# Dense columns stepped group by group, with two copies of the node features

## The reference

```
w  = edge_weight and 1 for each self loop
wn = w * rsqrt(deg_out[s]) * rsqrt(deg_in[d])
h  = x
repeat 10 times:                      # "steps"
    h = 0.9 * segment_sum(h[s] * wn, d) + 0.1 * x
x1 = layernorm(x + h)
score = exp(clip(sum_per_head(K[src] * Q[dst] * E / sqrt(8)), -5, 5))
out = layernorm(x1 + segment_sum(V[src] * score, dst))
```

## Time and profile before

| | |
|---|---|
| profiled execution | 13848.15 us |
| its span | 13846.3 us |
| median of the runs | 13851.04 us |
| TensorE (PE) busy | 73% of the span |
| GpSimd (POOL) busy | 64% |
| VectorE (DVE) busy | 41% |
| DMA read and written | 3177.87 MB and 303.14 MB |

### The profile page before, as it was taken

How to read it: one execution, slowest core, us unless ns; L and a number is a source line. 1 busy time by engine, 2 the same in 40 slices (tenths; PEclk the granted TensorE clock), 3 DMA queues, 4 the chain that set the end, 5 groups by cost and what they waited for, 6 DMA issues and landing times.

```text
span 13846.3 us, 141202 instructions
## 1 busy us (share of the span) xinstructions
PE 10055.4 (73%) x48612; PEld 5626.1 (41%) x48612; DVE 5672.0 (41%) x18837; ACT 688.7 (5%) x2111; POOL 8874.1 (64%) x8640
## 2 busy tenths in 40 slices
PE   0199994877868778688686886867868676777667
PEld 0199991332323323233232332333323355555555
DVE  6188881342333333333333333332333434444444
ACT  0033330000000000000000000000000010000000
POOL 3678887666666666666666666666666646666555
PEclk5555556988979889799797997989979855555555
DMA  9963335988969879699696996979969643333333
GB/s 394 385 165 69 69 54 174 374 296 310 375 228 374 328 273 375 227 375 363 236 376 231 373 374 225 373 265 336 377 228 374 249 110 108 113 109 110 106 105 97
DMA packets 1722567, 3491.10 MB, mean 252 GB/s; under 512 B 820288, under 2 KB 836067, under 8 KB 1721846
## 3 DMA queue, kind: packets, MB, share of 16 engines
q1 hardware_dynamic: 1145060, 2896.46, 56.9%
q0 software_dynamic: 379456, 296.48, 9.9%
q10 hardware_dynamic: 197330, 289.05, 5.8%
HBM read 3177.87 MB, written 303.14 MB: 251 GB/s over the span
## 4 chain that ended last, share of the span: by engine, by line
PE 55%; issue 15%; DVE 14%; another core or an unknown queue 8%; ACTq 5%; POOL 1%; ACT 1%; DMA 1%; DVEq 0%; SPq 0%
PE banks L1977 39%; PE banks L1996 5%; ACTq L1495 5%; PE banks L1946 4%; DVE arena L1673 2%; DVE arena L1737 2%; PE banks L1947 2%; PE banks L2067 1%; PE banks L2043 1%; DVE arena L1851 1%; PE banks L1989 1%; POOL dense L1460 1%; ACT arena L1504 1%; DVE arena L1687 1%
## 5 line engine op out<-in xcount | busy, mean ns | idle before, releaser
L1471 POOL DMA_INDIRECT arena<-node_rows,src_idx x5880 | 5623.7, 956 | 3174.3 <-issue 1655.0
L1977 PE MATMUL banks<-arena,u_sb 128*64 128x512 f32 x19600 | 5680.6, 625 | 1481.9 <-issue 1248.3
L1977 PEld LDWEIGHTS banks<-arena,u_sb 128*64 128x64 f32 x19600 | 1765.4, 142 | 4722.1 <-issue 4699.1
L1752 DVE TENSOR_TENSOR arena<-banks,arena 128x104 f32<-128x104 f32 (+20 forms) x1030 | 259.5, 257 | 5356.9 <-remote 4728.4
L1486 POOL DMA_INDIRECT arena<-kv_rows,src_idx x1568 | 1581.8, 1009 | 1136.8 <-DVEq L1910 553.0
L1737 DVE TENSOR_SCALAR arena<-banks,rel,w_tab 128x128 f32<-128x128 f32 x5880 | 1963.5, 403 | 166.5 <-issue 100.5
L1460 POOL DMA_INDIRECT dense<-arena x980 | 1633.5, 1667 | 591.9 <-issue 246.6
L1946 PE MATMUL banks<-arena 128*128 128x98 f32 x3136 | 1140.8, 467 | 694.8 <-ACT arena L1504 694.8
L1996 PE MATMUL banks<-arena 128*64 128x128 f32 x11760 | 1039.2, 301 | 661.6 <-issue 425.7
L1996 PEld LDWEIGHTS banks<-arena 128*64 128x64 f32 x11760 | 794.3, 149 | 925.0 <-issue 721.3
L1946 PEld LDWEIGHTS banks<-arena 128*128 128x128 f32 x3136 | 848.9, 331 | 702.9 <-ACT arena L1504 702.8
(11 more groups left out here) (166 smaller groups left out, 5382.1 us busy)
## 6 DMA issues: line engine op xcount, KB each, us to landing
arena<-dense SPq DMA_DIRECT2D x4900, 512.0 KB
dense<-blank ACTq DMA_DIRECT2D x5, 50176.0 KB, 371.2
arena<-in_dst_dram SPq DMA_DIRECT2D x195, 512.0 KB
arena<-node_rows,src_idx POOLq DMA_INDIRECT x5880
arena<-in_edge_attr_dram SPq DMA_DIRECT2D x195, 256.0 KB
u_sb<-key_rows SPq DMA_DIRECT2D x25, 1280.0 KB
u_sb<-in_edge_weight_dram SPq DMA_DIRECT2D x25, 1280.0 KB
arena<-key_rows SPq DMA_DIRECT2D x24, 1280.0 KB
```

Source lines behind the costliest of these rows:

```text
L1471: gp.indirect_dma_start(out=rows_in[:, n % ROWS, s, :], out_offset=None, in_=node_rows[k % 2], in_offset=bass.IndirectOffsetOnAxis(ap=src_ ...
L1977: last = mm(banks[h * D:(h + 1) * D, g, :], u_sb[:, j * D:(j + 1) * D], ring[:, u % SLOTS, h * 512:(h + 1) * 512], start=m < GROUPS, stop= ...
```

## The change

The dense part becomes 960 tiles and 4864 columns: four groups of 1024 columns and one of 768, of which only 768 columns are cleared, loaded and multiplied. The gathered part becomes 608 tiles, eight for each of 76 iterations. The ring has 14 slots, gathers may run 5 iterations ahead, the adds of setup go in 6 chunks, and the 490 units are spread over 74 of the 76 iterations. Units go group by group: all 98 blocks of group 0, then of group 1, and so on; each group sums in one of two banks in turn. Updates write a second copy of the features (`u_other`; the copies change places after every step), so a group is copied, turned and updated in the iteration after its last unit: iterations 15, 30, 45, 60 and 74. Within a group the blocks go 0 to 31, 38 to 97, and 32 to 37 last. ScalarE copies one bank for each group. Two waits for the adds of setup are new ahead of the steps, on GpSimd and on VectorE.

```diff
-DENSE_TILES = 980
-DENSE_COLS = 5120
+DENSE_TILES = 960
+DENSE_COLS = 4864
-TPI = 6
-SLOTS = 18
-ROWS = 7
-DENSE_ITERS = 84
+TPI = 8
+SLOTS = 14
+ROWS = 5
+DENSE_ITERS = 74
-CHUNKS = 7
+CHUNKS = 6
...
+    WIDTH = [min(GROUP, DENSE_COLS - g * GROUP) for g in range(GROUPS)]
-    dense_sum = carve(GROUPS, 512)
+    dense_sum = carve(2, 512)
+    u_other = carve(NB * D)
+    u_of = [u_sb[:, :], u_other]
...
-    GROUP_AT = {DENSE_ITERS + 2 * g: g for g in range(GROUPS)}
+    LAST_BLOCKS = list(GROUP_BLOCKS[-1])
+    BLOCK_AT = [b for b in range(NB) if b not in LAST_BLOCKS] + LAST_BLOCKS
+    UNIT = [(g, j) for g in range(GROUPS) for j in BLOCK_AT]
     UNIT_AT = [n * DENSE_ITERS // UNITS for n in range(UNITS)]
-    BLOCK_AT = [(i + DENSE_BLOCKS) % NB for i in range(NB)]
+    GROUP_AT = {UNIT_AT[(g + 1) * NB - 1] + 1: g for g in range(GROUPS)}
... run_sp
-                sp.dma_start(ring[:, n % SLOTS, :], dense_v[at:at + P, :]).then_inc(unit_loaded[n % SLOTS], 16)
+                sp.dma_start(ring[:, n % SLOTS, 0:WIDTH[g]], dense_v[at:at + P, 0:WIDTH[g]]).then_inc(unit_loaded[n % SLOTS], 16)
... run_pool, and the same in run_dve
+        for s in range(STREAMS):
+            pool.wait_ge(added[s], 16 * ROUNDS)
... run_act
-                    act.wait_ge(unit_used, (k + 1) * UNITS)
-                    for g in range(GROUPS):
-                        nc.scalar.activation(dense_sum[:, g, :], banks[:, g, :], ACT.Copy).then_inc(sum_copied, 1)
+                for turn, g in GROUP_AT.items():
+                    if turn <= i and g == copied:
+                        nth = k * GROUPS + g
+                        act.wait_ge(unit_used, k * UNITS + (g + 1) * NB)
+                        if nth >= 2:
+                            act.wait_ge(sum_turned, nth - 1)
+                        nc.scalar.activation(dense_sum[:, nth % 2, :], banks[:, nth % 2, :], ACT.Copy).then_inc(sum_copied, 1)
+                        copied += 1
... run_dve, update
-            u3 = by_node(u_sb, j0, j0 + m)
+            u3, new3 = by_node(u_of[k % 2], j0, j0 + m), by_node(u_of[(k + 1) % 2], j0, j0 + m)
-            return v.tensor_tensor(u3, part, o3, ALU.mult)
+            return v.tensor_tensor(new3, part, o3, ALU.mult)
... run_pe
-                    if k and m < GROUPS:
-                        pe.wait_ge(sum_read, (k - 1) * GROUPS + g + 1)
+                    if m % NB == 0 and nth >= 2:
+                        pe.wait_ge(sum_read, nth - 1)
-                        last = mm(banks[h * D:(h + 1) * D, g, :], u_sb[:, j * D:(j + 1) * D], ring[:, u % SLOTS, h * 512:(h + 1) * 512],
-                                  start=m < GROUPS, stop=m >= UNITS - GROUPS, tile_position=(0, h * D), skip_group_check=True)
+                        c = min(512, WIDTH[g] - h * 512)
+                        last = mm(banks[h * D:(h + 1) * D, nth % 2, 0:c], u_of[k % 2][:, j * D:(j + 1) * D], ring[:, u % SLOTS, h * 512:h * 512 + c],
+                                  start=m % NB == 0, stop=m % NB == NB - 1, tile_position=(0, h * D), skip_group_check=True)
```

More of the change, by code:

```diff
@@ L1048, in __init__ @@
         self.blank_set = sem("blank_set")
-        self.dense_cleared = [sem(f"dense_cleared{g}") for g in range(DENSE_COLS // GROUP)]
+        self.dense_cleared = [sem(f"dense_cleared{g}") for g in range(-(-DENSE_COLS // GROUP))]
         self.flag_ready = sem("flag_ready")
@@ L1085, in fast @@
     DENSE_BLOCKS = DENSE_COLS // P
+    assert DENSE_BLOCKS * P == DENSE_COLS and WIDTH[-1] > 512
+    GROUP_BLOCKS = [range(8 * g, min(8 * g + 8, DENSE_BLOCKS)) for g in range(GROUPS)]
     FIRST_BLOCK = BASE[DENSE_TILES // 2] // P
     LATE = DENSE_BLOCKS - FIRST_BLOCK
+    assert GROUP_BLOCKS[-1][0] <= FIRST_BLOCK < DENSE_BLOCKS
     assert ITERS * TPI == TILES - DENSE_TILES and ITERS % 2 == 0 and DENSE_TILES % 2 == 0
@@ L1317, in fast @@
     for n, (kind, i, what) in enumerate(UPDATES):
-        for b in (what if kind == "tail" else range(what * 8, what * 8 + 8)):
+        for b in (what if kind == "tail" else GROUP_BLOCKS[what]):
             UPDATED_AT[b] = n
-            last_use = max(UNIT_AT[m] for m in range(UNITS) if BLOCK_AT[m // GROUPS] == b)
-            assert last_use <= i - (kind == "dense")
     assert len(UPDATED_AT) == NB
@@ L1511, in run_act @@
         for k in range(STEPS):
[L1512 to L1515, removed]
+            to, u_new = node_rows[(k + 1) % 2], u_of[(k + 1) % 2]
+            copied = 0
             for n, (kind, i, what) in enumerate(UPDATES):
[L1517 to L1521 removed]
+                for turn, g in GROUP_AT.items():
[6 more added lines that the diff above has]
+                        copied += 1
                 if k + 1 == STEPS:
@@ L1757, in run_dve, with update @@
         step = Chain(dve, step_vec, fin.n)
-        def update(part, j0, m):
-            u3 = by_node(u_sb, j0, j0 + m)
+        def update(k, part, j0, m):
+            u3, new3 = by_node(u_of[k % 2], j0, j0 + m), by_node(u_of[(k + 1) % 2], j0, j0 + m)
             x3 = by_node(x_sb, j0, j0 + m)
@@ L1766, in update @@
             step(v.scalar_tensor_tensor(part, x3, ALPHA, part, ALU.mult, ALU.add))
-            return v.tensor_tensor(u3, part, o3, ALU.mult)
+            return v.tensor_tensor(new3, part, o3, ALU.mult)
+        for s in range(STREAMS):
+            dve.wait_ge(added[s], 16 * ROUNDS)
         hot_windows(0)
@@ L1788, in run_dve @@
                     if len(late) < len(done):
-                        last = update(parts[:, len(late):len(done), :], done[len(late)], len(done) - len(late))
+                        last = update(k, parts[:, len(late):len(done), :], done[len(late)], len(done) - len(late))
                         last.then_inc(updated, 1)
@@ L1797, in run_dve @@
                     dve.wait_ge(sum_turned, k * GROUPS + g + 1)
[L1798 to L1801, removed]
-                        step(v.tensor_tensor(part[:, b0:8, :], part[:, b0:8, :], carry[:, :, :], ALU.add))
-                    last = update(part, g * 8, 8)
+                    j0, m = GROUP_BLOCKS[g][0], len(GROUP_BLOCKS[g])
+                    part = banks[:, (k * GROUPS + g) % 2, 0:m * D].rearrange("p (j f) -> p j f", f=D)
+                    if g == GROUPS - 1:
+                        step(v.tensor_tensor(part[:, FIRST_BLOCK - j0:m, :], part[:, FIRST_BLOCK - j0:m, :], carry[:, :, :], ALU.add))
+                    last = update(k, part, j0, m)
                     last.then_inc(updated, 1)
-                    dve.wait_ge(updated, k * len(UPDATES) + UPDATED_AT[g * 8] + 1)
+                    dve.wait_ge(updated, k * len(UPDATES) + UPDATED_AT[j0] + 1)
                     dve.sem_inc(sum_read, 1)
```

22 lines of the change are left out of this document (13 added, 9 removed).

## The result

The kernel after took 14133.4 us (median of four runs, 14118.2 to 14143.5) beside 13848.7 for the kernel before: ratio 1.021 [1.020, 1.022]. The forecast was 12890 us, faster. The profiled execution had a span of 14133.2 us.

What follows compares the result with a forecast made beforehand. The prediction saw the bound pass from the loads to GpSimd's gathers: 2203.4 setup, nine steps of 791, a last one of 791 - 3.9, and 2774.7 behind gave 12884 us of span, forecast 12890; 8-in-10 range 12770 to 13190.

Steps and rivals of the forecast that it cites:

- setup: Ahead of the steps: 960 adds on GpSimd take 2034 us, so the first gather of step 0 comes at 2203.
- nine turns of a step: From first gather to first gather: 767 us of gathers, 6 of slip and 18 at the end, 791 us each.
- what lies behind: From the last update of step 9 to the kernel's end: 2774.7 us, untouched by the change.
- The step that failed: TensorE within a step: 7.0 us an iteration at 0.96 clock against 10.1 us of gathers, so not a bound.
- Start of a step: After the first gather: TensorE held until about 66 us, then catches up; GpSimd waits 6 us for room.
- slow spell: Some 20 us after gathers restart: TensorE's single matmuls 2.8 us apart for 47 us, cause unknown, expected at the same place.
- End of a step: After the last gather: its landing, three iterations and the stores, 18 us where the old wait is 34.
- DMA work: Loads, gathers and stores of one step on the DMA engines: 751 us before, 719 after.
- Gathers: GpSimd in each step: 608 gathers at 1.262 us make 767 us, a floor above the DMA work.
- Comparison with before: The old step of 883.2 us, read as a load-bound stretch of 725 plus a turn and a slow spell.
- B: Rival: a second slow spell in each step, 47 us more, 13360 us in all; chance 0.06.
- C: Rival: TensorE stays at its lower clock, 13.4 us an iteration at 0.50, 15000 us in all; chance 0.04.

Runs made afterwards that it cites:

- c1: The kernel before, unchanged, run again in the second set: 12336.9 us, beside 12331.7 us for the kernel before.
- c2: The kernel after, unchanged, run again in the second set: 12324.2 us, ratio 0.9993 to the kernel before.
- e14: The kernel after with 4 gathers instead of 8 in each iteration after the first five: 11136 us, 0.903 of the kernel before.
- e8: The kernel after with every unit's matmuls cut in eight, 64 columns each: 12763 us, beside 12330.7 us for the kernel before.

## Why the prediction was wrong

The sum of 12884 us of span against 14133.2, term by term: setup +8 (2203, 2211.7); nine turns of a step 9 x (914.0 - 791) = +1107; the last step 902 - 787 = +115; what lies behind +19. The error is in the step.

- **The step that failed: "TensorE. ... an iteration ... 7.0 us ... Not a bound at that clock."** The 7.0 us are right between the stretches, but three iterations take 35.0 us, 11.7 each, above the gathers' 10.1. I had divided busy rows by their count and left out what stood between them. The kernel before had the same 0.7 us gaps in every other iteration; its mean of a unit came from rows without gaps. Its steady part had them in this row, 105 us without a named cause in 700 (window 4960:5660):

```profile
L1977 PE MATMUL banks<-arena,u_sb 128*64 128x512 f32 x1859 | 526.2, 616 | 112.0 <-issue 105.1
```

There the loads, at a DMA share of 0.99, covered most of them. From the 26th to the 401st unit of a step (by the records, mean of steps 1 to 8) the kernel before takes 564 us with stretches and 535 without (c1), the kernel after 661 and 572 (c2): 30 us lost before, 88 after. The change took this cover away, and TensorE with its stretches, not GpSimd, set the pace.

- **Start of a step**: the slow spell stayed where it was, 45 us. But its slip of 6 us assumed that TensorE catches up at 7.0 us an iteration; GpSimd lost 131 us a step for room.
- **End of a step**: 31.9 us of waiting in each turn instead of 18, because TensorE is iterations behind. In c2, where it isn't, 18.5.
- **DMA work**, 719 us: too high. In e14 a step with loads as the bound takes 664; 304 gathers fewer explain 30 of the 55 (by my estimate of 0.099 us each). It decided nothing.
- **Gathers** (767) and **setup** (2203): right, 1.26 us each and 2211 us. In c2 the whole step is 783.9 for 791.
- **Comparison with before**: 883 us were taken as what loads and turn need. c1 needs 782.6 for the same program. In steps 1 to 8 the stretches cost the kernel before 103 us a step: 42 ahead of the 26th unit, 34 from there to the last one, 27 behind it. So even where my step came true nothing was won (0.9993), and its coming true there is no credit to the forecast of "faster".
- **Rivals**: none was it. B had the right object, further slow spells, but one a step, not some 25. C had the right engine at the wrong price: it stayed at the clock. The granted clock did fall (0.82 in the step's middle), but after TensorE had slowed down: in the trace it is 1.00 up to 4403, and 0.50, the lower of its two levels (1.2 GHz), from 4406 on. The Trainium skill, "TensorE: Matmul & The Clock Gate", section "HAM oscillation — how this bites in real kernels", says that waits between bursts of matmuls drop the clock and each burst then starts at the low one. The trace of c2 agrees in part: behind the wait of 3.75 us 28 records took 7.84 us, against 6.21 where there was no wait (4117.2). But its clock is 0.90 on average (3800 to 4500 us), and an iteration stays under the gathers' 10.1 us.

The link of the stretches to the loss is shown (the same two kernels with and without them). Their cause is open. One candidate can be set aside from the traces: TensorE's instructions are fetched in pieces of 16 KB (DMA queue q8, one for some 250 records), which took 1.07 us each after and 1.08 in c2, and the stretches begin anywhere from 0 to 30 us behind such a fetch. Load traffic, array work, gapless work and instruction rate were varied only where they don't occur, and no one of them brought them about. P rests on when they begin and end, and a pause of GpSimd can follow from TensorE's delay as well. Why some chips show them (two here, or three if the first comparison ran on another) and others (four) don't, no run tells; nor whether it is the chip itself or something else that differed between the sets. Of the chips on record only one was used in two sets, 75 minutes apart, and it was free of them both times.

## What to carry to other kernels

Divide a stretch by its iterations, not a busy row by its count; if the two differ and the gaps are put down to "issue", that time is a cost of the engine, and returns as soon as the engine that covered it gets faster. Ask for the profile on a second chip before pricing a change against a gap without a named cause. Where an order of work lets the engine with the floor (here GpSimd with the gathers) never wait, that gave 2% on chips without stretches; moving work onto that engine gave it back.

## What the runs showed of the hardware

- On some chips TensorE goes through stretches in which its instructions start 0.7 us or a multiple of it apart, 13 us long in every 35 (after). The same program (before) takes 12320 to 12332 us without and 13849 to 14000 us with them, 12% or more.
- The stretches are not TensorE's alone. SyncE issues its loads more slowly in them although the ring has room: by TensorE's records seven slots came free from 4394 to 4399 us, but the loads were issued at 4400.7, 4405.6, 4411.2 and 4413.3; in the long one at a step's start they are 11.2 us apart (4074.3, 4085.5, 4096.7, 4107.9), with the DMA engines at a share of 0.29. GpSimd's gathers keep their 1.26 us.
- The attention behind the steps suffers too: 2775 us with stretches, 2270 without (c1).
- TensorE took in 39 instructions per us over whole steps (e8) without any such stretch.
- A gather costs GpSimd 1.26 us in all of these traces, with and without stretches.
